# A decoder layer on one core: three turnings moved from TensorE to DMA, two bias rows moved from GpSimd to VectorE, and a new order inside the round

## The chip, the cores and the metric

The kernel runs on one core of one Trainium2 chip. The metric is the device time of the whole program in microseconds (us). The engines are named as the profile names them: PE is TensorE, DVE VectorE, ACT ScalarE, POOL GpSimd, and SP the engine that only issues DMAs. DMAs issued by SP travel in the queue called hardware_dynamic, those issued by POOL in software_dynamic; both are served by the same 16 DMA engines.

## The reference: what is computed

One post-norm decoder layer over x of 16 x 256 rows of 512 numbers: self-attention with 16 heads, cross-attention with one head of 64, then a mixture of 32 experts of which each token takes 8, with at most 512 tokens per expert.

```python
x = layernorm(x + attn(x))                    # softmax(q k^T / 8) v per head, then Wo, + bo
x = layernorm(x + xattn(ctx, ctx, x, mask))   # one head: out = softmax(q k^T / 8 - 1e9 mask) v; out @ Wo + bo
# experts
probs = softmax(x @ gate_weight.T); topw, topi = top_k(probs, 8); topw /= topw.sum(-1)
buf[e, pos] = x                               # up to 512 tokens for each expert
gate, up = split(buf @ gate_up_proj[e].T)     # 2 x 384
eo = (silu(gate) * up) @ down_proj[e].T
x = layernorm(x + sum over the 8 of topw * eo)
```

## The kernel before

Every matrix product is done in halves: a float32 number is written as a float16 high part plus a float16 low part (ACT makes the high part, DVE the low one, by `low` at L1107 to L1109, whose every use is profiled as L1109), and PE multiplies high with high, high with low and low with high, three products for one (`PARTS`, `split_mm` L508).

The program has two stages. The first is a software pipeline over the 16 batch elements, 19 rounds long (`rounds`, L330; rounds 4 to 14 are a loop on the engines, the others are written out). Round r works on four batch elements at once: b = r does q, k, v and the attention scores ("head"), t = r - 1 the rest of its heads, the projection and the first norm ("tail"), u = r - 2 the cross-attention and the second norm ("cross"), f = r - 3 the gate and the table of which token goes to which expert ("route"). So rounds 3 to 15 hold all four kinds of work, and rounds 16, 17 and 18 less and less. Each engine has its own `work` function with the whole round written out as eight steps of one head pair each; that order, by hand, is all the scheduling there is. An engine takes its instructions strictly in order, and a wait on a semaphore holds up all that stands behind it on that engine.

For a head pair j the chain is: `scores` (PE L550), `maxima` (DVE L1139), `exps` (ACT L863), `row_scales` (DVE L1145 and L1147), `probs_hi` (ACT L881), `probs_lo` (DVE, L1109 `stage<-arena_p`), `turn` (SP, two DMA transposes of 128 x 1024 float16, L402 and L404), `weigh` (PE L574), `heads_out` (ACT L853). The turning of the self-attention's probabilities and of x1 (`turn_x1`, L413 and L415) is done by DMA already. Three other turnings are done by PE against an identity matrix, out of float32: the cross-attention's probabilities (`cross_turn`, L623, 4 blocks of 128 x 128), x2 for the gate (`turn_x2`, L645, 8 blocks), and the gathered tokens of an expert (`turn_xg`, L775, 16 blocks). After each, ACT and DVE take the result out of PSUM as high and low half (`turned2_hi` L918 and `turned2_lo`; `x2_turned` L942 and `x2_lo`; `tokens_hi` L1057 and `tokens_lo`).

Two bias rows are added on POOL: `add_bias` (L1573, to xr, which holds the residual rows) and `add_bias2` (L1583, to x1). POOL's other work in a round is the low half of q and k (`qk_low`, L1564) and of the head outputs (`heads_lo`, L1568).

The second stage goes over the 32 experts. PE does `up_gate` (72 matmuls of 512 columns, L512), two blocks of `turn_xg` for the next expert, and `down` (36 matmuls, L786) with the two other blocks between its parts. POOL gathers the rows of expert e + 2 from x2_rows by indirect DMA (`gather`, L1654, 4 DMAs), and adds the 4 results of expert e into acc_rows by indirect DMA (`scatter`, L1660). SP loads the weights of expert e + 2 (`load_expert`, L418 and L420). The tokens of an expert stay in `xg` (two buffers, float32), their turned halves in `xgT` (one buffer, in `arena_v`). Before the first expert's matmuls PE does `turn_xg` four times with `keep_warm` matmuls (L678) between.

A third, short stage normalizes the 4096 rows.

## Time and profile before

| | us |
|---|---|
| median of 3 runs | 2085.09 (2084.96 to 2090.12) |
| the profiled execution | 2086.91 |
| its span in the profile | 2085.2 |
| PE, DVE, ACT, POOL busy in the span | 1879.4, 1421.7, 1258.3, 828.5 |
| mean granted clock of PE | 0.957 |

The span is the time from the first to the last instruction in the trace; about 1.7 us of the execution lie outside. Times inside the trace are us from the start of the span. The stage of rounds lasts until about 1214 us, the experts from about 1225 to 2037, and the last norm to the end. "Busy" is time with at least one instruction running; a busy engine can still be one that waits inside an instruction, for a port or an operand. The chain of work that ended last is 57% PE and 23% DVE, and PE is busy 90% of the span.

### The profile page before, as it was taken

What the parts mean: (1) busy time and instruction counts of PE and PEld (TensorE: products, weight loads), DVE (VectorE), ACT (ScalarE), POOL (GpSimd) and SP (SyncE); (2) the same over time, 40 slices, a digit from 0 to 9 for tenths busy, and PEclk for the clock granted to TensorE, in tenths of its full rate; (3) what the DMA queues carried; (4) which work ended last, traced back from release to release, by engine and by line L of the source; (5) the groups of instructions that cost most, each with busy time, mean ns of one, the idle gap of its engine ahead of it and who ended that gap; (6) DMA issues with size and microseconds to landing.
All of it is one profiled execution on the core that took longest, in us unless ns stands there. A gap on an engine that the chain in (4) does not pass through costs nothing.

```text
span 2085.2 us, 41762 instructions
## 1 busy us (share of the span) xinstructions
PE 1879.4 (90%) x14388; PEld 1113.9 (53%) x14388; DVE 1421.7 (68%) x2665; ACT 1258.3 (60%) x3119; POOL 828.5 (40%) x703
## 2 busy tenths in 40 slices
PE   6899999999999999999997559999999999999990
PEld 4556666566666665666564334444444444444440
DVE  5667898889888988898888655544555554555534
ACT  6877787778777877787776224444444444444434
POOL 1323332334233323332333135555555555555522
PEclk9999999999999999999998679999999999999995
DMA  7654554455445543554446157777777777777639
GB/s 214 127 99 104 109 128 111 90 112 125 106 91 112 122 111 81 122 122 109 86 111 143 51 176 220 178 178 178 178 176 175 180 180 189 189 189 179 130 46 336
DMA packets 418729, 295.26 MB, mean 142 GB/s; under 512 B 318704, under 2 KB 341232, under 8 KB 418672
## 3 DMA queue, kind: packets, MB, share of 16 engines
q1 hardware_dynamic: 389728, 224.26, 40.8%
q0 software_dynamic: 28944, 70.27, 18.2%
q8 instruction: 32, 0.52, 0.1%
q14 instruction: 25, 0.20, 0.0%
HBM read 158.67 MB, written 60.29 MB: 105 GB/s over the span
## 4 chain that ended last, share of the span: by engine, by line
PE 57%; DVE 23%; issue 10%; ACT 7%; DMA 1%; POOL 1%; DVEq 1%; ACTq 0%; SPq 0%; POOLq 0%
PE bank L512 39%; PE bank L786 12%; DVE stage L1109 7%; DVE s_neg L1139 5%; PE bank L775 3%; ACT arena_p L863 2%; PE bank L574 1%; DVE neg_l L1266 1%; PE bank L550 1%; ACT qk L843 1%; ACT arena_wo L1099 1%; DVE xt L1109 1%; DVE ct L1109 1%; DVE x1h L1109 1%; DVE stats L1175 1%
## 5 line engine op out<-in xcount | busy, mean ns | idle before, releaser
L512 PE MATMUL bank<-arena_v,arena_wo 128*128 128x512 f16 x2304 | 502.5, 379 | 0.6 <-PE bank L678 0.6
L512 PE MATMUL bank<-xt,arena_wo 128*128 128x256 f16 x3072 | 369.2, 278 | 18.8 <-DVE xt L1109 10.4
L512 PEld LDWEIGHTS bank<-arena_v,arena_wo 128*128 128x128 f16 x2304 | 225.3, 98 | 273.1 <-PE bank L678 1.5
L512 PEld LDWEIGHTS bank<-xt,arena_wo 128*128 128x128 f16 x3072 | 298.6, 100 | 84.5 <-issue 22.1
L1660 POOL DMA_INDIRECT acc_rows<-arena_wo,cur_to x128 | 202.4, 1581 | 308.3 <-ACT arena_wo L1079 276.9
L1109 DVE SCALAR_TENSOR_TENSOR arena_wo<-stage,arena_wo 128x3072 f16<-128x3072 f32 (+2 forms) x74 | 182.2, 2465 | 190.9 <-ACT arena_wo L936 174.9
L1564 POOL TENSOR_TENSOR qk<-qk 128x512 f16<-128x512 f32 x128 | 164.9, 1288 | 341.7 <-ACT qk L843 332.0
L863 ACT ACTIVATE arena_p<-bank,s_neg 128x256 f32<-128x256 f32 x512 | 236.2, 484 | 78.5 <-DVE s_neg L1139 78.5
L1109 DVE SCALAR_TENSOR_TENSOR stage<-arena_p,s_rden,stage 128x256 f16<-128x256 f32 x512 | 276.9, 600 | 5.7 <-ACT stage L881 5.7
L786 PE MATMUL bank<-arena_wo 128*128 128x512 f16 x1152 | 264.2, 379 | 0.7 <-DVE arena_wo L1511 0.7
L1568 POOL TENSOR_TENSOR arena_a<-o,arena_a 128x256 f16<-128x256 f32 x128 | 97.5, 762 | 384.9 <-ACT arena_a L853 383.9
L881 ACT ACTIVATE stage<-arena_p,s_rden 128x256 f16<-128x256 f32 x512 | 220.8, 527 | 36.8 <-DVE s_rden L1147 36.3
L1654 POOL DMA_INDIRECT arena_p<-x_rows,cur_from x128 | 214.9, 1679 | 56.2 <-issue 29.2
L843 ACT ACTIVATE qk<-bank,bqkv 128x256 f32<-128x256 f32 (+1 forms) x512 | 203.0, 502 | 44.6 <-PE bank L512 44.2
L1109 DVE SCALAR_TENSOR_TENSOR arena_v<-bank,arena_v 128x512 f16<-128x512 f32 x192 | 129.4, 687 | 105.2 <-ACT arena_v L1057 91.0
L1067 ACT ACTIVATE arena_a<-bank 128x512 f32<-128x512 f32 x96 | 57.0, 594 | 235.8 <-PE bank L512 235.8
L1079 ACT ACTIVATE arena_wo<-bank,cur_w 128x512 f32<-128x512 f32 x128 | 87.9, 687 | 162.2 <-PE bank L786 162.2
L512 PE MATMUL bank<-arena_wo,xt 128*128 128x512 f16 x768 | 178.0, 382 | 1.9 <-DVE arena_wo L1109 1.9
L1139 DVE TENSOR_REDUCE s_neg<-bank 128x2 f32<-128x512 f32 x256 | 163.7, 679 | 22.8 <-PE bank L550 22.8
L512 PE MATMUL bank<-arena_wo,arena_a 128*128 128x512 f16 x768 | 172.9, 382 | 2.2 <-POOL arena_a L1568 2.2
L786 PEld LDWEIGHTS bank<-arena_wo 128*128 128x128 f16 x1152 | 110.7, 98 | 117.9 <-DVE arena_wo L1511 10.4
L1504 DVE SCALAR_TENSOR_TENSOR arena_a<-bank,arena_a 128x512 f32<-128x512 f32 x96 | 65.9, 687 | 122.0 <-PE bank L512 121.7
(152 smaller groups left out, 2489.1 us busy)
## 6 DMA issues: line engine op xcount, KB each, us to landing
stage<-wguT SPq DMA_DIRECT2D x32, 1536.0 KB, 8.5
stage<-wdnT SPq DMA_DIRECT2D x32, 768.0 KB, 9.8
xt<-xT SPq DMA_DIRECT2D x16, 512.0 KB, 4.4
xr<-x_rows SPq DMA_DIRECT2D x16, 512.0 KB, 3.7
stage<-ctxT SPq DMA_DIRECT2D x16, 512.0 KB, 4.0
x_rows<-x SPq DMA_DIRECT2D x16, 512.0 KB, 2.9
acc_rows<-x SPq DMA_DIRECT2D x16, 512.0 KB, 3.7
arena_wo<-acc_rows SPq DMA_DIRECT2D x8, 1024.0 KB, 11.1
```

Source lines behind the costliest of these rows:

```text
L512: mm = pe.matmul(out_ap, lhs(a, i), rhs(c, i), start=(n == 0 and i == 0), stop=(n == 2 and i == chunks - 1))
L786: mm = pe.matmul(ps_y[c % 2][:, :], hT[:, a, f, c * P:(c + 1) * P], ew_dn[:, k, w, f, :], start=(f == 0 and n == 0), stop=(f == FC - 1 and ...
L843: ins = nc.scalar.activation(dst, ps_qk[:, at], ACT.Identity, bias=bqkv[:, w, j:j + 1], scale=scale / W_SCALE)
L863: ins = nc.scalar.activation(probs[:, j % 2, h, t, :], ps_s[h][:, t * S:(t + 1) * S], ACT.Exp, bias=s_neg[:, j % 2, n:n + 1], accum_out=s_ ...
L881: ins = nc.scalar.activation(p16[:, j % 2, 0, n * S:(n + 1) * S], probs[:, j % 2, n // TT, n % TT, :], ACT.Identity, scale=s_rden[:, j % 2 ...
L1079: nc.scalar.activation(y[:, k, c, :], ps_y[c % 2][:, :], ACT.Copy, scale=cur_w[:, k, c:c + 1]).then_inc(y_done, 1)
L1109: return vec.scalar_tensor_tensor(out=dst, in0=src, scalar=scale, in1=hi, op0=ALU.mult, op1=ALU.subtract)
L1139: vec.tensor_reduce(s_neg[:, j % 2, 2 * h:2 * h + 2], ps_s[h][:, :].rearrange("p (t k) -> p t k", t=TT), AX.X, ALU.max, negate=True).then_ ...
L1564: gp.tensor_tensor(qk[:, j % 2, 1, :], qk32[:, j % 2, :], qk[:, j % 2, 0, :], ALU.subtract).then_inc(qk_lo, 1)
L1568: gp.tensor_tensor(o[:, 1, j, :], o32[:, j % 2, :], o[:, 0, j, :], ALU.subtract).then_inc(o_lo, 1)
L1654: gp.indirect_dma_start(xg[:, k, c, :], None, x2_rows, bass.IndirectOffsetOnAxis(ap=cur_from[:, k, c:c + 1], axis=0)).then_inc(ld_xg[k], 16)
L1660: gp.indirect_dma_start(acc_rows, bass.IndirectOffsetOnAxis(ap=cur_to[:, k, c:c + 1], axis=0), y[:, k, c, :], None, compute_op=ALU.add).th ...
```

## The change

First, the three turnings on PE go. The data is split into halves before it is turned, lies as float16 in SBUF, and SP turns it with DMA transposes. For the cross-attention's probabilities ACT and DVE write `p2h` (128 x 512 each), SP turns it into `p2T` with 2 transposes of 4 blocks. For x2 they write `x2h`, and 2 transposes of 8 blocks make `x2T`. The rows of x2 are then stored to DRAM as halves (`x2_halves`), so that the gathered tokens are halves already, and 4 transposes of 8 blocks per expert turn them; ACT and DVE have nothing to split there. The turned tokens have two buffers (`xgT[k]`), and the results of `down` four PSUM banks where they had two. The `keep_warm` matmuls before the first expert go too. The division by the softmax sum of the cross-attention, a DVE pass over p2, is folded into the scale of the two splits.

```diff
-        xgT = arena_v[:, :].rearrange("p (s c n) -> p s c n", s=2, c=DC)
+        xg16 = arena_p[:, :].bitcast(F16).rearrange("p (b c n) -> p b c n", b=2, c=CC)
+        xgT = [arena[:, :].rearrange("p (c s d n) -> p c s d n", c=CC, s=2, d=DC) for arena in (arena_v, arena_q)]
...
-        ps_y = bank[6:8]
+        ps_y = bank[4:8]
...
+            def turn_halves(b, dst, src, done, free, free_at, landed):
...
+                sp.wait_ge(done[0], high)
+                past(sp, free, used)
+                sp.dma_start_transpose(dst[:, 0].rearrange("p t c n -> p (t c) n"), src[:, 0, :]).then_inc(landed, 16)
+                wait_apart(sp, done[1], count(b, 1, 1), ld_bias, 48)
+                sp.dma_start_transpose(dst[:, 1].rearrange("p t c n -> p (t c) n"), src[:, 1, :]).then_inc(landed, 16)
...
+            def turn_tokens(e, k, gathered):
+                landed, used = gathered, count(e - 1, FC)
...
+                sp.wait_ge(ld_xg[k], landed)
+                past(sp, u_mm, used)
+                for c in range(CC):
+                    sp.dma_start_transpose(xgT[k][:, c].rearrange("p s d n -> p (s d) n"), xg16[:, k, c, 0:2 * D])\
+                      .then_inc(ld_xgt[k], 16)
...
+            def tokens_then_weights(e, k, gathered):
+                turn_tokens(e, k, gathered)
+                next_but_one(e, 1 - k)
...
-            def expert(e, k, ahead, landed):
-                up_gate(e, k)
-                if ahead:
-                    pe.wait_ge(ld_xg[1 - k], landed)
-                    turn_xg(e + 1, 1 - k, 0)
-                    turn_xg(e + 1, 1 - k, 1)
-                down(e, k, ahead)
-
-            pe.wait_ge(ld_xg[0], 64)
-            for c in range(CC):
-                turn_xg(0, 0, c)
-                if c % 2:
-                    keep_warm(WARM[1])
+            def expert(e, k, landed):
+                up_gate(e, k, landed)
+                down(e, k)
...
+            def split_x2(b):
+                past(act, ld_x2t, count(b, 32))
+                past(act, st_x2, count(b, 48))
+                act.wait_ge(x2_done, count(b, TT, TT))
+                nc.scalar.activation(x2h[:, 0, :], x2[:, :, :].rearrange("p t n -> p (t n)"), ACT.Copy).then_inc(x2_hi, 1)
...
+            def split_p2(b):
+                dve.wait_ge(p2_hi, count(b, 1, 1))
                 for t in range(TT):
-                    ins = vec.tensor_scalar(p2[:, t, :], p2[:, t, :], rden2[:, t:t + 1], None, ALU.mult)
-                ins.then_inc(p2_done, 1)
+                    at = slice(t * S, (t + 1) * S)
+                    ins = low(p2h[:, 1, at], p2[:, t, :], p2h[:, 0, at], rden2[:, t:t + 1])
+                ins.then_inc(p2_lo, 1)
```

Second, the two bias rows. The same addition over 128 x 1024 float32 numbers is written for DVE in place of POOL.

```diff
+            def add_bias(b):
+                if isinstance(b, int) and b == 0:
+                    dve.wait_ge(ld_small, 32)
+                dve.wait_ge(ld_row, count(b, 16, 16))
+                vec.tensor_tensor(xr[:, :, :], xr[:, :, :], bo_row[:, :].unsqueeze(1).to_broadcast([P, TT, D]), ALU.add)\
+                   .then_inc(xb_done, 1)
+
+            def add_bias2(b):
+                past(dve, x1_lo, count(b, 1, 1))
+                vec.tensor_tensor(x1[:, :, :], x1[:, :, :], xbo_row[:, :].unsqueeze(1).to_broadcast([P, TT, D]), ALU.add)\
+                   .then_inc(x1b_done, 1)
```

Third, the order of the round on all engines, with the PSUM banks that go with it. On PE in the loop (the middle of a round, before): the turning of p stands behind the values' matmuls, and the pieces of the cross-attention lie between the two halves of the projection, `bank<-arena_wo,arena_a`.

```order
182 L512 MATMUL bank<-arena_wo,xt 128x512 x12
183 L620 REGISTER_ALU
184 L623 MATMUL bank<-ident,p 128x128 x4
185 L550 MATMUL bank<-qk 128x256 x12
186 L574 MATMUL bank<-arena_p,arena_v 64x256 x12
187 L52 REGISTER_ALU
188 L512 MATMUL bank<-xt,arena_wo 128x256 x24
189 L522 MATMUL bank<-p2T,v 64x256 x6
190 L588 REGISTER_ALU
191 L512 MATMUL bank<-arena_wo,arena_a 128x512 x24
192 L550 MATMUL bank<-qk 128x256 x12
193 L512 MATMUL bank<-wxo,o 128x512 x3
```

The same place after, where `arena_q` is the arena that now holds q and k:

```order
178 L586 MATMUL bank<-arena_q 128x256 x12
179 L610 MATMUL bank<-arena_p,arena_v 64x256 x12
180 L52 REGISTER_ALU
181 L548 MATMUL bank<-xt,arena_wo 128x256 x24
182 L548 MATMUL bank<-arena_wo,arena_a 128x512 x24
183 L586 MATMUL bank<-arena_q 128x256 x12
184 L548 MATMUL bank<-arena_wo,arena_a 128x512 x24
185 L604 REGISTER_ALU
186 L605 REGISTER_ALU
187 L610 MATMUL bank<-arena_p,arena_v 64x256 x12
188 L659 REGISTER_ALU
189 L558 MATMUL bank<-p2T,v 64x256 x6
```

There is no turning, and the product with p2T has moved behind the whole projection.

On ACT at the start of a round in the loop, before (`stage<-arena_p` are the high halves of the probabilities, `o<-bank` a head's output, `x1h` the high half of x1, `qk<-bank` what takes q and k out of PSUM):

```order
201 L826 ACTIVATE xt<-xt 128x1024
202 L878 ISA
203 L879 ISA
204 L881 ACTIVATE stage<-arena_p,s_rden 128x256 x4
205 L52 ISA
206 L851 REGISTER_ALU
207 L853 ACTIVATE o<-bank,bqkv 128x256
208 L853 ACTIVATE arena_a<-bank,bqkv 128x256
...
211 L889 ACTIVATE x1h<-x 128x1024
...
214 L863 ACTIVATE arena_p,s_den<-bank,s_neg 128x256 x4
...
217 L843 ACTIVATE qk<-bank,bqkv 128x256 x4
```

And after:

```order
200 L828 ACTIVATE xt<-xt 128x1024
...
203 L883 ACTIVATE stage<-arena_p,s_rden 128x256 x4
...
206 L865 ACTIVATE arena_p,s_den<-bank,s_neg 128x256 x4
...
209 L855 ACTIVATE o<-bank,bqkv 128x256
210 L855 ACTIVATE arena_a<-bank,bqkv 128x256
...
214 L947 ACTIVATE stage<-x 128x1024
...
217 L845 ACTIVATE arena_q<-bank,bqkv 128x256 x4
...
220 L891 ACTIVATE x1h<-x 128x1024
```

The exponentials come before the head's output, the split of x2 (`stage<-x`) is new and stands before what frees the PSUM bank of q and k, and the split of x1 has moved behind it.

On SP at the start of a round, after: the transposes of x2 stand between those of a head pair and those of x1.

```order
108 L404 DMA_TRANSPOSE arena_p<-stage 128x8x128
109 L406 DMA_TRANSPOSE arena_p<-stage 128x8x128
110 L412 ISA
111 L416 DMA_TRANSPOSE stage<-stage 128x8x128
112 L418 DMA_TRANSPOSE stage<-stage 128x8x128
113 L412 ISA
114 L416 DMA_TRANSPOSE x1T<-x1h 128x8x128
115 L418 DMA_TRANSPOSE x1T<-x1h 128x8x128
```

Before, the second pair of rows is not there.

## Rows read from the trace of the kernel before

**Rows 1.** Stretches: all experts but the edges, ten rounds; busy of each engine, clock, DMA

```profile
1231.00:2010.00 779.00, 779.00 (x3855) 382.02 (x3856) 401.64 (x465) 323.75 (x403) 425.86 (x334) 1.00 0.71 174
...
343.20:1043.50 700.30, 654.58 (x6510) 443.25 (x6507) 602.03 (x1291) 547.83 (x1662) 233.96 (x200) 0.99 0.49 109
```

**Rows 2.** Timeline of PE and SP's issues, two experts: start, us, what

```profile
1522.11 1.04 PE L775 MATMUL bank<-ident,arena_p 128*128 128x128 f32 x8
1522.98 2.11 PE L786 MATMUL bank<-arena_wo 128*128 128x512 f16 x9
...
1517.35 0.37 SPq L418 DMA_DIRECT2D stage<-wguT  x1
...
1542.42 0.37 SPq L418 DMA_DIRECT2D stage<-wguT  x1
```

**Rows 3.** DMA queues over one expert, 1506.57 to 1531.64: packets, MB, share of 16 engines

```profile
q0 software_dynamic: 896, 2.16, 47.8%
q1 hardware_dynamic: 928, 2.36, 26.6%
```

**Rows 4.** DMA queue from 613.5 to 616.5, one transpose alone

```profile
q1 hardware_dynamic: 1056, 0.26, 45.7%
```

**Rows 5.** DMA queues: 1507 to 1510 (scatter alone), then 1261 to 1264 (with loads)

```profile
q0 software_dynamic: 196, 0.37, 94.5%
...
q0 software_dynamic: 133, 0.25, 49.1%
```

**Rows 6.** Who PE waited for in ten rounds: us in total, times, longest

```profile
PE bank L623 <- DVE p L1224: 17.7, 10, 1.9
```

**Rows 7.** Timeline of PE, turnings in a round, and the clock from 656 to 660

```profile
621.44 1.04 PE L645 MATMUL bank<-ident,x 128*128 128x128 f32 x8
622.41 1.76 PE L671 MATMUL bank<-stage 128*32 128x16 f16 x64
...
655.64 0.66 PE L623 MATMUL bank<-ident,p 128*128 128x128 f32 x4 [1.94 <-DVE p L1224]
656.23 0.96 PE L550 MATMUL bank<-qk 64*128 64x256 f16 x12
...
656.00:660.00 4.00, 4.00 (x34) 2.52 (x33) 4.00 (x5) 4.00 (x10) 2.31 (x1) 0.60 0.84 197
```

**Rows 8.** Groups of DVE in ten rounds: busy, mean ns, idle before

```profile
L1109 DVE SCALAR_TENSOR_TENSOR x1h<-x,x1h 128x1024 f16<-128x1024 f32 x10 | 12.1, 1211 | 0.0
L1109 DVE SCALAR_TENSOR_TENSOR p2T<-bank,p2T 128x512 f16<-128x512 f32 x10 | 6.8, 680 | 0.0
L1224 DVE TENSOR_SCALAR p<-p,rden 128x256 f32<-128x256 f32 x20 | 6.2, 350 | 0.4
```

**Rows 9.** Timeline of DVE and POOL: where a POOL addition and DVE overlap

```profile
628.50 1.79 DVE L1109 SCALAR_TENSOR_TENSOR stage<-arena_p,s_rden,stage 128x256 f16<-128x256 f32 x4
...
631.67 2.21 DVE L1266 TENSOR_SCALAR neg_l<-top_l 128x2 f32<-128x2 f32 x1
...
644.41 4.18 DVE L1109 SCALAR_TENSOR_TENSOR stage<-arena_p,s_rden,stage 128x256 f16<-128x256 f32 x4
...
645.77 2.54 POOL L1573 TENSOR_TENSOR xr<-xr,bo_row 128x1024 f32<-128x1024 f32 x1
```

**Rows 10.** Issue to landing of a transpose; timeline of x1's two and their user

```profile
arena_p<-stage SPq DMA_TRANSPOSE x256, 3.1
...
631.88 1.24 SPq L413 DMA_TRANSPOSE x1T<-x1h  x1
633.28 1.24 SPq L415 DMA_TRANSPOSE x1T<-x1h  x1
...
639.10 0.85 PE L522 MATMUL bank<-x1T,wx 128*64 128x256 f16 x12
```

**Rows 11.** Start of the experts: timeline of PE, and its clock from 1225 to 1231

```profile
1224.96 1.97 PE L775 MATMUL bank<-ident,arena_p 128*128 128x128 f32 x8 [11.39 <-DMA arena_p<-x_rows,cur_from]
...
1225.00:1231.00 6.00, 5.39 (x21) 3.68 (x22) 2.92 (x5) 3.25 (x5) 2.83 (x7) 0.56 0.89 300
```

More of the change, by code:

```diff
@@ L637, in cross_project, with gate @@
                     .then_inc(out2_mm, 1)
-            def turn_x2(b, t, tail):
-                pe.wait_ge(x2_done, count(b, TT, t + 1))
-                if t and tail:
+            def gate(b, tail):
+                pe.wait_ge(ld_x2t, count(b, 32, 32))
+                if tail:
                     pe.wait_ge(ln1, count(b + 1, 7, 1))
-                for c in range(DC):
-                    mm = pe.transpose(ps_x2[t][:, c * P:(c + 1) * P], x2[:, t, c * P:(c + 1) * P], ident[:, :])
-                mm.then_inc(x2t_mm, 1)
@@ L704, in work @@
                     qk_pair(b, 2)
-                if route:
-                    positions(f)
+                    values(b, 1)
                 if cross:
```

432 lines of the change are left out of this document (194 added, 238 removed).

## The prediction

> **What bounds the kernel now.** I read the stretches first. In the 779 us of the experts PE is busy for 779 of 779 us at full clock, with DVE, ACT and POOL at about half and the DMA engines at 0.71 [rows 1]. So what PE is given there is the time, and nothing else is. In ten rounds (700.3 us, 70.03 each) PE is busy 654.6, DVE 602.0, ACT 547.8, POOL 234.0 [rows 1]: PE leads, with 4.57 us idle per round, and DVE is close behind at 60.2 per round. Then the waits of PE: 1.77 us per round for the scaled p that it turns [rows 6]. That hole costs more than itself: in the 4 us behind it the granted clock has a mean of 0.60, part of it at the lower of the two levels, 1.2 in place of 2.4 GHz [rows 7], and 4 x 0.40 = 1.6 us of work is lost. Then the timeline of DVE beside that of POOL: the same four probability splits take 1.79 us alone and 4.18 us when POOL's addition to xr (2.54 us) runs beside them, and a neg_l of 128 x 2 numbers takes 2.21 us where POOL adds the other bias row [rows 9]. The 4.18 stand ahead of the masking, and so of the hole. Last the DMA queues, since that is where the work goes.
>
> **The experts.** Eight turnings start at 1522.11 and the next product at 1522.98: 0.87 us [rows 2]. 16 per expert make 1.74 us. The period is 1542.42 - 1517.35 = 25.07 us [rows 2]; without the turnings 23.33. There are 31 such sets between the experts (the first expert's is in the start, below): 31 x 1.74 = -53.9 us. ACT and DVE lose four passes each; they had half their time free, so that is worth nothing.
>
> Does something else become late? Each expert gets 4 transposes of 256 KB. One alone takes 0.457 x 3 x 16 = 21.9 engine-us, four 87.7 [rows 4]. Today one expert takes (0.478 + 0.266) x 25.07 x 16 = 298 [rows 3]. The sum, 386, over 16 engines is 24.1 us, and this is above 23.33. But POOL's packets are long because they wait alone: 0.945 x 48 us / 196 = 231 ns for one of the scatter with the queue to itself, and 0.491 x 48 / 133 = 177 ns where weight loads run beside it [rows 5]. If the 192 engine-us of that queue shrink in that proportion to 147, the sum is 342 or 21.3 us, under 23.33. So bounds 23.33 and 24.1; I take 23.33, since the engines, once short of time, are in the mixed state. Late arrivals are forgiven: the gather of expert e + 2 is issued early in expert e, its transposes may start when e's 72 matmuls are done, and they are needed one expert later, with two buffers. SP issues them at 1.40 us spacing [rows 10], 5.6 us of 23.3, and its load of the next weights, which it issues once per expert, comes between them without waiting for more than today. For POOL's gather the wait on a landed turning is for one issued an expert before.
>
> The Trainium skill (Advanced Engine Details and Errata, X-Bar Transpose (TRN2)) says that transposing DMAs are as fast as regular ones. Rows 3 and 4 do not agree: 2.36 MB of weights take 107 engine-us, 45 per MB, a transpose 84 per MB. By the rule the four would cost about 47 and the experts' sum without any shrinking would be 345, 21.6 us; by the rows the case is close.
>
> **The rounds.** PE loses 4 turnings of p (656.23 - 655.64 = 0.59 us) and 8 of x2 (0.97) [rows 7]: 1.56. With the hole's clock loss of 1.6 gone, PE's work is 65.46 - 1.56 - 1.6 = 62.3 us: the floor. Idle today is 4.57, of which 1.77 is the wait for the turned p. In the new order the product with p2T stands behind the whole projection and one head pair; from the end of the splits two transposes need 1.40 + 3.1 = 4.5 us [rows 10], and the projection's second half and a pair's work lie over them, so I count no wait. The other 2.8 us stay. I add 1.0 for ACT: its new split of x2 (the size of DVE's 1.21 [rows 8]) stands ahead of what empties the only bank of q and k, and PE's values no longer stand behind the first q and k, so the second must wait for the bank. 62.3 + 2.8 + 1.0 = 66.1 us against 70.03: -3.9. Bounds: 62.3, and 68.5 if all the idle time and the clock loss come back elsewhere (62.3 + 4.57 + 1.6).
>
> DVE decides whether that holds. It loses 0.68 for p2T, two of that size for x2, and 0.62 for the scaling [rows 8]: 2.7. It gains a split of x2 (1.21), two of the four splits of 1.79 us for p (0.9), a scaling of two numbers (under 0.35) and two additions of 128 x 1024. No row has these on DVE: the nearest from below is the split of the same size, 1.21, from above POOL's 2.54; I take 1.2 each, the row of the same engine. Sum +4.7. And the stalls beside POOL's additions go: 4.18 - 1.79 = 2.4, and 2.21 against at most the 0.35 of the much larger scaling [rows 8], 1.9: -4.3, down to 0 if POOL's remaining work hits DVE instead. The edits come to +2.0, so DVE ends at 60.2 + 2.0 - 4.3 = 57.9, at the worst (2.54 each, no stall back) at 64.9. At 57.9 it covers; at 64.9 the round is some 68. On SP each round gets 4 transposes more, 5.6 us; x1's two now come behind x2's two, 2.8 us later. They landed by 633.28 + 3.1 = 636.4 and were needed at 639.10 [rows 10]: 2.7 of slack, and the gate and a block of values now stand ahead of that product.
>
> Rounds 2 to 15 have this work in full or nearly: 14 x -3.9 = -55 us. POOL's queue gets shorter; that hides nothing.
>
> **Start and tail.** The first gather lands at 1224.96, and PE's own turning and warm-up lasted until about 1231, at a mean granted clock of 0.56 [rows 11]. After: four issues and a landing, 3 x 1.40 + 3.1 = 7.3, so matmuls from 1232.3, +1.3; and they begin after 19 us without work, so at the lower level, as the turnings did. The half speed then falls on matmuls, for about the 6 us of that row: 6 x 0.44 = +2.6. Together +4. In rounds 16 to 18 nothing covers the transposes: for p about 4.5 us of DMA replace PE, ACT and DVE passes (0.59, and two of the size of 0.68, with gaps), roughly +2 twice, for x2 +1.5 twice, less 1.2 twice for the addition that DVE does faster than POOL: +4.
>
> **Sum.** Against the profiled execution, 2086.9 (span 2085.2 and 1.7 around it): 2086.9 - 53.9 - 55 + 4 + 4 = 1986. The median shown is 1.8 lower: **1984 us**, 4.8% less.
>
> **Rivals.**
> A, the rounds keep their time. DVE is at its worst, or ACT's new order makes PE wait for the bank or for the exponentials what it saves. For it: DVE is 86% busy, and each engine now has its pieces in an order in which one late piece holds up the next head pair. Against: the stalls it loses are in the rows. 1984 + 55 = 2039 us.
> B, the DMA engines set the experts' pace without shrinking: 24.1 us and some gaps, up to 24.8. 31 x 0.8 to 1.5 = +25 to +46, so about 2020.
> C, x1T is late: its transposes behind x2's, and both splits later in ACT and DVE than I laid them. 2.8 us per round, 14 x 2.8 = +39: 2023.
> D, slower than before: transposes of 256-byte packets get slower beside scatter and gather rather than these shorter. The experts lose once the four cost more than 25.07 x 16 - 298 = 103 engine-us, 26 each against 21.9 alone; only 19% more. At half as much again (33 each) the engines need 430, 26.9 us: +1.8 x 31 = +56 where I have -54, so 1984 + 110 = 2094; to be over 2085 they must reach 32. For it: so many packets; against: the mixed rows.
> E, the floor is reached in the rounds (62.3 to 64): 1984 - 14 x 3 = 1942.
>
> The Trainium skill (VectorE: DVE Perf Modes, The three transpose paths and its rules for kernel authors) gives 390 ns for a 128 x 128 block on TensorE and 1309 ns by DMA, and advises TensorE where the result may be in PSUM. It speaks against the change. The trace shows the same sign for latency (3.1 us for a transposing DMA, 0.11 of PE per block), but where PE is full its 0.11 is what counts; taken as it stands, the rule would have the change at best in case A or C.
>
> **How the numbers follow.** Forecast 0.52 (1965 to 2005), A 0.12, B 0.11, C 0.08, D 0.09, E 0.08. The range 1945 to 2050 leaves out most of D and part of E, with the worse part of A and B: 0.2. About 0.3% is what a measurement can tell from no change: faster 0.88, same 0.03, slower 0.09, D with a small part of A and B together as "same".
>
> **What would show it.** Right: in the experts PE busy all the time at full clock and the weight loads 23.3 us apart; DMA share near 0.9 to 0.95; rounds of 65 to 67 us; neg_l back under 0.35 us and no split of 4 us; PE's wait for turned p gone, at most small ones before the second q and k and the exponentials. Wrong: PE waiting for `xgT` (B, D); a POOL packet that has not become shorter; PE waiting for x1T (C), or DVE over 64 us busy in a round (A).

## The result and the profile after

The changed kernel takes 2040.9 us (2036.19 to 2044.33, four runs) where the kernel before takes 2085.95 in the same comparison: a ratio of 0.9774, interval 0.9763 to 0.9786. Faster, as forecast, but by 45 us and not by 101; 2040.9 lies in the range. It is near the time of rival A by chance: A has the rounds keep their time, but half of what is missing was lost in the experts. The profiled execution took 2036.19 with a span of 2034.1 us.

| part | before | forecast | after |
|---|---|---|---|
| one expert, load to load | 25.07 | 23.33 | 24.16 |
| one round (issue of xr to issue of xr) | 69.90 | 66.1 | 67.93 |
| PE busy in a round | 65.5 | 62.3 | 63.6 |
| end of the last slots matmul to first expert matmul | 17.4 | 18.7 | 23.8 |

The stretches of the changed kernel, ten rounds and then 600 us of experts, answer to [rows 1]; the columns are the same (busy time and instructions of PE, PE's weight loads, DVE, ACT, POOL, then the clock, the DMA share and GB/s):

```profile
286.80:966.10 679.30, 635.91 (x6378) 432.33 (x6377) 564.19 (x1299) 546.75 (x1657) 177.57 (x179) 0.99 0.57 124
1300.00:1900.00 600.00, 583.69 (x2687) 260.72 (x2685) 257.42 (x272) 210.68 (x224) 377.97 (x275) 1.00 0.97 230
```

DVE is at 56.4 us per round, under the 57.9 of the forecast. PE, busy without a gap among the experts before, now idles 16.3 us in 600. The waits of PE tell what for. First the experts (1200 to 1990; us in total, times, longest), and then the ten rounds:

```profile
PE bank L548 <- DMA arena_v<-arena_p: 23.8, 1, 23.8
PE bank L802 <- DVE arena_wo L1509: 21.7, 32, 0.7
```

```profile
PE bank L586 <- ACT arena_p L865: 24.9, 20, 2.1
PE bank L548 <- ACT arena_q L845: 13.4, 10, 1.3
PE bank L548 <- DVE xt L1098: 2.8, 10, 0.3
```

The one wait for turned rows is the start, 23.8 us. The other is new: 0.68 us in each of 32 experts, in front of `down`'s products with the last third of h (the 384 rows of an expert's hidden values h are handled as three blocks, f = 0, 1, 2). The timeline of PE and of SP's issues over one expert shows its place, and the period (24.15 us here, 24.16 in the mean):

```profile
1465.17 1.46 PE L802 MATMUL bank<-arena_wo 128*128 128x512 f16 x6
1467.30 6.65 PE L802 MATMUL bank<-arena_wo 128*128 128x512 f16 x30 [0.68 <-DVE arena_wo L1509]
...
1460.42 0.38 SPq L441 DMA_DIRECT2D stage<-wguT  x1
1469.51 7.46 SPq L437 DMA_TRANSPOSE arena_v<-arena_p  x4
...
1484.57 0.38 SPq L441 DMA_DIRECT2D stage<-wguT  x1
```

`down` needs h of the last f, and its low half is ready some 2 us after the last up matmul. Before, eight turnings lay between them [rows 2]. The trace of before had this hole in PE's work too, in its last expert, which has no next one to turn:

```profile
2025.38 6.65 PE L786 MATMUL bank<-arena_wo 128*128 128x512 f16 x30 [0.68 <-DVE arena_wo L1511]
```

The DMA queues of the changed kernel over one expert, 1460.42 to 1484.57, against [rows 3]:

```profile
q1 hardware_dynamic: 5152, 3.41, 61.3%
q0 software_dynamic: 903, 2.19, 40.0%
```

POOL's packets take 0.400 x 24.15 x 16 us / 903 = 171 ns, where before they took 0.478 x 25.07 x 16 / 896 = 214. They shrank, as the forecast had it. The other queue has 237 engine-us; less the 107 of the weights [rows 3], that leaves 32 per transpose, against 21.9 alone [rows 4], if the weights cost what they did. Both queues overlap to a share of about 1, yet no expert but the first waits for a transpose.

In the rounds the two long stalls on DVE are gone and the additions cost what I took. These are DVE's neg_l, a set of its four splits of p and its two additions, against 2.21 and 4.18 us in [rows 9]:

```profile
553.10 0.17 DVE L1267 TENSOR_SCALAR neg_l<-top_l 128x2 f32<-128x2 f32 x1
...
564.21 1.68 DVE L1098 SCALAR_TENSOR_TENSOR stage<-arena_p,s_rden,stage 128x256 f16<-128x256 f32 x4
...
566.09 1.22 DVE L1162 TENSOR_TENSOR x<-x,xbo_row 128x1024 f32<-128x1024 f32 x1
...
578.64 1.22 DVE L1157 TENSOR_TENSOR xr<-xr,bo_row 128x1024 f32<-128x1024 f32 x1
```

PE still waits 4.1 us in a round (4.3 with the smallest gaps), with other waits than in [rows 6]. The largest is ahead of scores(2), the scores of head pair 2. Its chain, read from PE back to ACT and to DVE's routing choice (whose last instruction is w), with what POOL does beside w:

```profile
565.54 0.83 PE L586 MATMUL bank<-arena_q 64*128 64x256 f16 x12 [1.97 <-ACT arena_p L865]
...
561.24 1.71 ACT L883 ACTIVATE stage<-arena_p,s_rden 128x256 f16<-128x256 f32 x4 [1.21 <-DVE s_rden L1136]
...
559.78 1.07 DVE L1292 SCALAR_TENSOR_TENSOR w<-pr,w_rsum 128x64 f32<-128x64 f32 x1
560.78 0.17 DVE L1134 RECIPROCAL s_rden<-s_den 128x4 f32<-128x4 f32 x1
```

```profile
559.62 1.16 POOL L1556 TENSOR_TENSOR arena_q<-arena_q 128x512 f16<-128x512 f32 x1 [2.61 <-ACT arena_q L845]
```

So one stretched DVE instruction is left in this chain. w takes 1.07 us in all ten rounds, and 0.23 in the last round, where POOL has nothing beside it; here it ends where POOL's low half of q and k ends. The kernel before had the same (w 1.04 us). No run parted the two.

The clock did not come back whole either. Ten us around the wait before scores(2), in two rounds that follow each other (the clock is the third figure from the end):

```profile
495.00:505.00 10.00, 8.29 (x60) 5.29 (x61) 7.94 (x23) 9.64 (x34) 2.55 (x3) 0.83 0.45 85
...
565.00:575.00 10.00, 9.46 (x74) 5.72 (x75) 8.37 (x23) 10.00 (x34) 2.57 (x3) 1.00 0.52 98
```

The first round has a dip to the lower level behind that wait, the second has none. Five of the ten rounds have one, and they take 68.6 to 69.0 us; those without take 67.2 to 67.5, the first of the ten 65.9.

### The profile page after: what moved, and what is told of

The parts are those of the page before. It is cut to its first block, busy times and chain, and to the rows that moved or that the text cites. A ratio compares the mean times of both kernels' runs of the same rounds, so it can differ in the third digit from the quotient of the medians.

```text
span 2034.1 us, 40256 instructions
## 1 busy us (share of the span) xinstructions
PE 1793.0 (88%) x13680; PEld 1034.9 (51%) x13680; DVE 1283.1 (63%) x2553; ACT 1192.3 (59%) x2991; POOL 766.5 (38%) x669
## 4 chain that ended last, share of the span: by engine, by line
PE 54%; DVE 17%; ACT 15%; issue 9%; DMA 2%; SPq 1%; POOL 1%; DVEq 1%; ACTq 0%; POOLq 0%
PE bank L548 40%; PE bank L802 10%; ACT arena_p L865 4%; DVE stage L1098 3%; ACT stage L883 3%; ACT arena_q L845 3%; DVE s_neg L1128 2%; PE bank L586 2%; PE bank L610 1%; ACT arena_wo L1088 1%; DVE arena_wo L1509 1%; DVE arena_a L1502 1%; ACT arena_a L855 1%; DVE ct L1098 1%; DVE xt L1098 1%
## 5 line engine op out<-in xcount | busy, mean ns | idle before, releaser
L1556 POOL TENSOR_TENSOR arena_q<-arena_q 128x512 f16<-128x512 f32 x128 | 168.6, 1317 | 370.9 <-ACT arena_q L845 354.5
L802 PE MATMUL bank<-arena_wo 128*128 128x512 f16 x1152 | 259.4, 379 | 21.7 <-DVE arena_wo L1509 21.7
L548 PE MATMUL bank<-arena_v,arena_wo 128*128 128x512 f16 x1152 | 253.5, 381 | 23.8 <-DMA arena_v<-arena_p 23.8
L1560 POOL TENSOR_TENSOR arena_a<-o,arena_a 128x256 f16<-128x256 f32 x128 | 91.2, 712 | 455.8 <-ACT arena_a L855 455.8
L1098 DVE SCALAR_TENSOR_TENSOR stage<-arena_p,s_rden,stage 128x256 f16<-128x256 f32 x512 | 230.8, 510 | 39.8 <-ACT stage L883 39.8
L548 PE MATMUL bank<-arena_q,arena_wo 128*128 128x512 f16 x1152 | 251.3, 379 | 0.0
L845 ACT ACTIVATE arena_q<-bank,bqkv 128x256 f32<-128x256 f32 (+1 forms) x512 | 203.9, 507 | 55.4 <-PE bank L548 55.4
L883 ACT ACTIVATE stage<-arena_p,s_rden 128x256 f16<-128x256 f32 x512 | 221.0, 532 | 16.3 <-DVE s_rden L1136 16.3
L548 PEld LDWEIGHTS bank<-arena_v,arena_wo 128*128 128x128 f16 x1152 | 113.2, 98 | 161.3 <-DMA arena_v<-arena_p 23.9
L1632 POOL DMA_INDIRECT arena_p<-x_rows,cur_from x128 | 164.6, 1286 | 56.4 <-issue 29.0
L548 PEld LDWEIGHTS bank<-arena_q,arena_wo 128*128 128x128 f16 x1152 | 112.7, 98 | 135.9
```

Of the source, the lines that this page charges most:

```text
L548: mm = pe.matmul(out_ap, lhs(a, i), rhs(c, i), start=(n == 0 and i == 0), stop=(n == 2 and i == chunks - 1))
L802: mm = pe.matmul(ps_y[c][:, :], hT[:, a, f, c * P:(c + 1) * P], ew_dn[:, k, w, f, :], start=(f == 0 and n == 0), stop=(f == FC - 1 and n = ...
L845: ins = nc.scalar.activation(dst, ps_qk[:, at], ACT.Identity, bias=bqkv[:, w, j:j + 1], scale=scale / W_SCALE)
L883: ins = nc.scalar.activation(p16[:, j % 2, 0, n * S:(n + 1) * S], probs[:, j % 2, n // TT, n % TT, :], ACT.Identity, scale=s_rden[:, j % 2 ...
L1098: return vec.scalar_tensor_tensor(out=dst, in0=src, scalar=scale, in1=hi, op0=ALU.mult, op1=ALU.subtract)
L1556: gp.tensor_tensor(qk[:, j % 2, 1, :], qk32[:, j % 2, :], qk[:, j % 2, 0, :], ALU.subtract).then_inc(qk_lo, 1)
```

## The experiments

Each was timed beside the kernel before, whose median was 2085.5 us beside e1 to e4, 2088.1 beside e5 to e8, 2087.83 beside e9 to e11 and 2087.06 beside e12 to e15. Periods come from the profiled runs: of a round from ten rounds between SP's issues of xr, of an expert from its weight loads or from PE's first matmul.

| run | us | ratio (interval) | round | expert |
|---|---|---|---|---|
| changed kernel | 2040.9 | 0.9774 (0.9763-0.9786) | 67.93 | 24.16 |
| e1 down's order | 2011.23 | 0.9668 (0.9625-0.9711) | 67.87 | 23.31 |
| e2 quarter turned | 2065.33 | 0.9903 (0.9887-0.992) | | 24.38 |
| e3 scales first | 2041.73 | 0.978 (0.9763-0.9797) | 67.85 | |
| e4 x2 after qk | 2042.03 | 0.9788 (0.9772-0.9804) | 68.16 | |
| e5 ring first | 2014.13 | 0.9648 (0.9632-0.9664) | 67.47 | |
| e6 half the turning | 2011.33 | 0.9634 (0.9618-0.965) | 67.94 | 23.31 |
| e7 biases on POOL | 2080.9 | 0.9969 (0.9959-0.9979) | 71.39 | |
| e8 biases alone | 2027.18 | 0.9708 (0.9692-0.9724) | 65.69 | |
| e9 ring then qk | 2024.31 | 0.9701 (0.9685-0.9717) | 68.55 | |
| e10 norm later | 2007.11 | 0.9619 (0.9603-0.9635) | 67.09 | |
| e11 start too | 2003.24 | 0.9599 (0.958-0.9618) | 67.13 | |
| e12 values back | 2011.45 | 0.9643 (0.9627-0.9659) | 67.44 | |
| e13 and norm later | 1995.73 | 0.9588 (0.9552-0.9624) | 65.94 | |
| e14 and x2 early | 1986.44 | 0.9532 (0.951-0.9554) | 65.70 | |
| e15 with start | 1987.64 | 0.9552 (0.9503-0.9601) | 65.75 | |

**e1, down's order.** The changed kernel, with `down` beginning on the two thirds of h that are ready, for two of its four blocks of rows c:

```diff
-for c in range(CC):
-    for f in range(FC):
+order = [(0,0), (1,0), (0,1), (1,1), (0,2), (1,2)] + [(c,f) for c in (2,3) for f in range(FC)]
+for c, f in order:
```

> The changed kernel with one edit: in down, PE does the first and second third (f = 0, 1) of both c = 0 and c = 1 before the last third of either, so 12 matmuls (2.6 us) stand between up_gate and the first use of h's last third, where the changed kernel has 6 (1.3 us). Theory H: the turnings on PE had covered the way from the last up_gate matmul over ACT's silu and DVE's three passes to h's last low half, and their removal uncovers a hole of 0.68 us per expert; it goes: experts 23.48 us apart, 32 x 0.68 = 22 us less than the changed kernel, about 2019 us, ratio to before 0.968. Rival D: the DMA engines, 0.97 busy in the experts, are what sets 24.16 us; then the period stays near 24.1, a wait for the turned tokens takes the hole's place, and the ratio stays 0.977.

The hole is gone. Experts of e1, 600 us of them, and PE over one expert:

```profile
1300.00:1900.00 600.00, 600.00 (x2781) 272.02 (x2780) 268.23 (x284) 215.00 (x232) 359.08 (x286) 1.00 1.02 239
```

```profile
1526.42 7.93 PE L803 MATMUL bank<-arena_wo 128*128 128x512 f16 x36
1534.19 15.70 PE L548 MATMUL bank<-arena_v,arena_wo 128*128 128x512 f16 x72
```

The period is 23.31, the forecast's 23.33, with PE full and the DMA engines at 1.02. So the lost 0.85 us per expert was this hole: 0.68 shown as idle and 0.17 of the pipeline that empties ahead of it (7.93 us for the 36 matmuls against 1.46 + 0.68 + 6.65 with their overlap at the ends). 31 x 0.85 = 26 us, which is the difference of the two spans (2034.1 and 2008.0).

**e2, a quarter of the turnings.** The kernel before, with one block of four turned for every group of rows (three quarters of the rows' columns are left out of the computation):

```diff
-for d in range(DC):
+for d in range(1):   # all but the first expert
```

> The kernel before with one edit: of the 16 blocks that PE turns per expert (from the second expert on) it turns only 4, one per group of rows; the other three quarters of the tokens are left out of the turning. No DMA is added. By the sum of the prediction this is worth 12 x 0.109 = 1.3 us per expert, 31 times, 40 us, ratio 0.981. Theory H says that 0.65 us of it fall on the 2 blocks-groups between up_gate and down, which cover the last low half of h: 6 matmuls and 2 blocks give 1.5 us where about 2.0 to 2.15 are needed, so a hole of 0.5 to 0.65 us per expert opens, and only about 0.7 to 0.8 us per expert remain: 23 us, ratio 0.989, experts 24.3 us apart with full DMA slack.

```profile
1465.99 0.82 PE L786 MATMUL bank<-arena_wo 128*128 128x512 f16 x3 [0.46 <-DVE arena_wo L1511]
```

Twelve of the sixteen blocks are worth 12 x 0.109 = 1.31 us of PE, but the period falls only by 0.69, to 24.38: the hole opens in the kernel before as soon as the turnings shrink. The row shows 0.46 us of it; with the same 0.17 for the emptying pipeline as in e1 it is 0.63, and e1's 23.31 with that and four turnings (0.44) makes 24.38, as measured.

**e3 and e4, single moves in the changed kernel.** e3 put the scaling of pair 0 ahead of the routing's choice on DVE, e4 ACT's and DVE's split of x2 behind the copy of the first q and k:

```diff
e3 (DVE)                          e4 (ACT; DVE alike)
-if route: choose(f)              -if route: split_x2(f)
 pair(row_scales, 0)               if head: qk_out(b, 0)
+if route: choose(f)              +if route: split_x2(f)
```

> The changed kernel with one edit: on DVE the row scales of pair 0 stand ahead of the choice of the experts (choose, 11 small operations, some 3.2 us), which in the changed kernel stands ahead of them. Theory O: ACT's high halves of pair 0 wait 1.2 us for those scales, behind them stand the exponentials of pair 1, and PE waits 1.97 us for them at the scores of pair 2. The wait goes nearly whole: rounds of 66.0 to 66.5 us in place of 67.93, 14 x 1.6 = 22 us, about 2019 us, ratio 0.968. Rival: the hole is DVE's total load, not its order; then the scores' wait moves to another place and the rounds stay within 0.4 us of 67.93.

> The changed kernel with one edit: ACT's split of x2 stands behind the taking out of the first q and k instead of before it, and DVE's split of x2 behind the row scales. Theory O: PE's wait of 1.34 us per round for the bank of q and k is that split's 1.08 us; it falls to about 0.3: rounds of 66.9, 14 x 1.0 = 14 us, about 2027 us, ratio 0.971. Rival C: x2T and x1T, turned later by the same amount, are late for the gate and the cross-attention's q, the wait moves there and nothing is won (ratio 0.977).

Neither changed the time: both rivals held. In e3 ACT started the high probabilities 1.2 us earlier, but then waited 1.17 us for the maxima, which still stood behind the choice. In e4 the waits for ACT fell, and PE waited for transposes instead (ten rounds of e4, their stretch first):

```profile
289.60:971.20 681.60, 645.06 (x6375) 433.94 (x6373) 566.23 (x1298) 552.38 (x1658) 179.86 (x180) 0.97 0.57 124
```

```profile
PE bank L558 <- DMA x1T<-x1h: 17.6, 10, 1.8
PE bank L548 <- DMA stage<-stage: 5.8, 10, 0.7
PE bank L586 <- ACT arena_p L865: 4.9, 10, 0.5
PE bank L548 <- ACT arena_q L845: 3.9, 10, 0.4
```

So case C of the prediction lies just behind the order as it is: with the splits 1.6 us later on ACT, x1T is late. But PE idles only 3.7 us in a round of e4, against 4.3 in the changed kernel. What took the gain back is the clock: every round now has a dip, behind the wait for x1T, and PE is busy for 64.5 us in place of 63.6 with the same work.

**e5, the ring first.** The ring is scores, maxima (DVE), exps (ACT), and the next scores into the bank that the exps empty. On the kernel of e1:

```diff
DVE: row_scales(0), maxima(1)                       ACT:  +exps(1)
     ahead of values_lo(1) and choose                      heads_out(-2)
                                                           probs_hi(0)
                                                          -exps(1)
```

> The kernel with down's order from e1, and in the step of the second scores the ring scores, maxima, exps goes ahead: on VectorE the maxima(1) stand before the low half of the values and the routing's choice, on ScalarE the exps(1) stand before the heads of pair -2 and the high probabilities of pair 0. Theory R: the hole of 2.0 us that TensorE has in every full round before scores(2) is made by 3.4 us of choice and 0.7 us of low half that stand ahead of the maxima, and by 2.6 us of ScalarE's work ahead of the exps; e3 moved only a scaling of 0.4 us and left the choice ahead of the maxima, so it gained nothing. Then the hole goes, a round takes 66.0 to 66.5 instead of 67.9 us, and the time is 1985 to 1992. Rival S: ScalarE and VectorE are so full that the wait comes back at the next scores or at the turned probabilities: a round stays over 67.3, 2003 to 2015.

The wait before scores(2) went, and one of nearly that size came at the next product, which needs q and k's bank:

```profile
574.94 2.79 PE L548 MATMUL bank<-xt,arena_wo 128*128 128x256 f16 x24 [1.59 <-ACT arena_q L847]
```

Rival S holds, with 67.47 a round. PE's waits are no shorter than in e1 (4.1 us in a round in both); the 0.4 us are the clock's, since no round of e5 has a dip. The first rounds lost 8 us besides, so that the profiled execution is 4 us longer than e1's (2014.23 and 2010.1).

**e6, half the turning.** e1 with only the high halves turned; the matmuls take the high half in the place of the low one.

> The kernel of e1 with only the high halves of the gathered rows turned, and the high half taken in the place of the low one in the matmuls (a part of the computation left out): half of the transposed bytes in every expert, the same matmuls. Theory: in e1 TensorE is busy in 600 of 600 us of experts, so the DMA engines at a share of 1.02 do not set the pace and a period stays 23.3; what shrinks is the start, where the turning stands between the gathers and the first matmul with 10.6 us to land: to 6 or 7 us, 2005 to 2008 against e1's 2011. Rival B (DMA engines at their limit cost time somewhere in the experts' loop): a period under 23.2, over 5 us below the start's gain, under 2000.

No change: the experts stay 23.31 us apart with PE busy in 600 of 600 us, though the DMA share fell to 0.89. None at the start either. The first four transposes with half the bytes took 1196.33 to 1205.6, against 1195.28 to 1205.1: it is not their size that they wait for. Rival B is out; my 3 to 6 us for the start were wrong as well.

**e7 and e8, the two halves of the change apart.** e7 is the changed kernel with the two additions back on POOL, e8 the kernel before with only the two additions on DVE, in the same steps of the round as in the changed kernel.

> The changed kernel with the two bias rows added by GpSimd again, at their places of the kernel before; everything else as changed. By the sum of the prediction the DVE instructions that stood beside GpSimd's additions were stretched by 2.2 and 4.2 us in a round and TensorE waited for them: if that was worth time, a round is 1 to 2.5 us longer, 2055 to 2075. Rival W: TensorE's wait of 4.3 us in a round is set by the ring of scores, maxima and exps with the choice in it, which no bias touches: within 5 us of the changed kernel's 2041.

> The kernel before with only the biases moved to VectorE, as the changed kernel has them; TensorE still turns. VectorE gains two additions of 1.2 us in a round and loses the stretching beside GpSimd. By the sum: a round shorter by what it made TensorE wait, up to 2 us, 2060 to 2080. Rival W: no more than 3 us either way, 2083 to 2089. Rival D: the additions on VectorE stand ahead of maxima, a round longer by 0.5 to 1, 2092 to 2100.

e8 beats the whole change: 61 us under before against 45, and e7, all the rest, has 7. Both effects are over what I expected (28 us at most for e8, 34 for e7 over the changed kernel). Ten rounds of e8 and e7, then the two large PE waits of before in its ten rounds, then those of e8 and of e7:

```profile
286.60:943.60 657.00, 643.33 (x6502) 439.26 (x6500) 564.27 (x1310) 547.26 (x1660) 186.53 (x180) 1.00 0.52 116
```

```profile
288.20:1002.10 713.90, 646.54 (x6378) 437.30 (x6377) 581.90 (x1278) 547.03 (x1658) 228.69 (x200) 0.96 0.54 118
```

```profile
PE bank L550 <- ACT arena_p L863: 18.2, 10, 1.8
PE bank L623 <- DVE p L1224: 17.7, 10, 1.9
```

```profile
PE bank L512 <- DVE slots L1345: 4.9, 10, 0.5
PE bank L512 <- DVE xt L1109: 3.7, 10, 0.4
PE bank L512 <- POOL arena_a L1582: 2.1, 10, 0.2
PE bank L550 <- ACT arena_p L863: 1.7, 10, 0.2
```

```profile
PE bank L586 <- ACT arena_p L865: 48.8, 20, 4.9
PE bank L548 <- ACT arena_q L845: 13.4, 10, 1.3
```

| a round, us (PE busy + idle) | biases on POOL | on DVE |
|---|---|---|
| old order, PE turns | 69.90 (65.5 + 4.4) | 65.69 (64.3 + 1.4) |
| new order, DMA turns | 71.39 (64.7 + 6.7) | 67.93 (63.6 + 4.3) |

The additions' move is worth 3.5 to 4.2 us in a round in either order: 2.4 to 3.0 of waits, and 1.1 to 1.2 of PE's busy time, though PE's work is the same; that part is the clock (0.96 and 0.99 in the new order, 0.99 [rows 1] and 1.00 in the old). The rest of the change costs 1.5 to 2.2. It does take about 1.5 us of work off PE: e14 below, like e8 at a clock of 1.00, is busy for 62.9 us in a round, where e8 has 64.3. But in the changed kernel 0.7 of that goes to its dips in the clock, and 3.0 us of idle time come on top. In e8 no wait of PE is over 0.5 us: the two large ones of before (1.8 before a scores, 1.9 before the turned p) went with the additions, as the DVE instructions of [rows 9] that had been stretched beside them did, and the clock rose to 1.00. In e7 the stretched one stands inside the choice, here POOL's addition and DVE's w (1.95 us at the median of ten rounds, for the 0.23 without POOL beside it), and PE's wait behind it:

```profile
576.06 2.35 POOL L1551 TENSOR_TENSOR xr<-xr,bo_row 128x1024 f32<-128x1024 f32 x1 [2.28 <-DMA xr<-x_rows]
```

```profile
576.54 1.94 DVE L1281 SCALAR_TENSOR_TENSOR w<-pr,w_rsum 128x64 f32<-128x64 f32 x1
```

```profile
583.94 0.83 PE L586 MATMUL bank<-arena_q 64*128 64x256 f16 x12 [4.50 <-ACT arena_p L865]
```

The Trainium skill (SBUF — State Buffer, Who interferes with whom) says that DVE's second pair of ports is GpSimd's too, and that a use of it locks the other engine out. The trace agrees as far as the times go: 1.94 us for one of 0.23, and w ends 0.07 us behind the addition beside it.

**e9 to e11, on the ring again.** e9 moves qk_out(3) ahead of the high probabilities in e5; e10 puts DVE's norm1 of a block behind the next round's first maxima, where the kernel before and the changed one have it at the end of a round; e11 adds the start: the second gather behind the first turning, and 14 idle matmuls on PE.

```diff
e10 (DVE)                         e11 (POOL; on PE keep_warm(14) before expert 0)
-if tail: norm1(t)    # round's end       -gather(1, 1)
 ...                                       column_out(0, 0)
 pair(maxima, -2); pair(probs_lo, -3)     +pool.wait_ge(ld_xgt[0], 64)
+if cross: norm1(u)   # next round        +gather(1, 1)
```

> As e5, but on ScalarE the copy of the next queries and keys, qk_out(3), stands between the heads of pair -2 and the high probabilities of pair 0 (the first round keeps its old order, since e5 lost 8 us there). e8 showed a round of 65.7 with the biases on VectorE and TensorE still turning, 2.2 less than the changed kernel's 67.9, though TensorE works 0.7 more in it: theory O says that those 2.2 and more are made by the new order of the rounds, not by turning by DMA. e5 took the wait of 2.0 us before scores(2) away and got 1.6 us back at qk_pair(4), behind 1.7 us of high probabilities. By theory O that wait goes too: a round takes 65.8 to 66.3, 1982 to 1990. Rival S: ScalarE is late again one step on, a round stays over 67.2, 2000 to 2012.

> As e9, and VectorE's normalization of the first residual (two instructions, 1.0 to 1.9 us) moved from the end of a round to the start of the next, behind the maxima of pair -2. By theory O the 0.5 and 1.3 us that TensorE waits at a round's border come from exps that wait 2.55 us for these maxima: a round of 64.2 to 64.8, 1958 to 1970, TensorE's waits under 1.2 us in a round. Rival: the low half of x1, and with it cross_q, comes late instead: no change against e9 or up to 1 us a round worse.

> As e10, and between the rounds and the experts: the gather of the second expert is issued only when the turning of the first has landed, and TensorE does 14 idle matmuls while the first is turned (the kernel before had such matmuls there). e6 halved the bytes turned and the four transposes still took 9.3 us from first issue to landing, against 9.8, so bytes are not what they wait for. If it is the second expert's gather and the weights on the same engines, the start shortens by 3 to 5 us, and the first 72 matmuls take 15.7 in place of 17.2 to 18.6: 4 to 7 us under e10. Rival: the transposes cost 2 us each to issue whatever runs beside them: 1 to 2 us from the clock alone.

e9 missed: 68.55 a round, worse than e1, and rival S holds. The wait moved on once more, to the low half of a head on POOL and to o, the output of the cross-attention:

```profile
647.45 5.35 PE L548 MATMUL bank<-arena_wo,arena_a 128*128 128x512 f16 x24 [1.24 <-POOL arena_a L1567]
664.18 1.47 PE L548 MATMUL bank<-wxo,o 128*128 128x512 f16 x6 [1.34 <-DVE o L1103]
```

e10 took 1.46 off, as forecast, though from e9's higher level, so its 67.09 misses the 64.2 to 64.8. e11 took 3.9 us off e10 (2003.24 and 2007.11), just under the 4 to 7 expected: the first expert started 3.8 us earlier, with all 72 matmuls at full clock,

```profile
1199.07 15.70 PE L548 MATMUL bank<-arena_v,arena_wo 128*128 128x512 f16 x72 [2.60 <-issue]
```

and 2.4 came back at the fifth expert, whose turning was late.

**e12 to e15, the filler put back.** On e1, the second quarter of the values (12 matmuls, 2.75 us) goes behind qk_pair(3), with its copies, where the kernel before has it (e12); norm1 as in e10 (e13); ACT's high half of x2 at the end of the round (e14); the start of e11 (e15):

```diff
e12 (PE; ACT and DVE alike)       e14 (ACT)
 qk_pair(b, 2)                    -if route: split_x2(f)    # before qk_out(0)
-values(b, 1)                      ...
 ...                               qk_out(b, 7)
 qk_pair(b, 3)                    +if cross: split_x2(u)    # end of the round
+values(b, 1)
```

> The kernel of e1 with the second quarter of the values, 2.75 us of TensorE, and its two copies put back one step later, where the kernel before and e8 have them (behind qk_pair(3)). Theory V: in the changed order TensorE has 8.0 us of work in one step and 4.5 in the next, while ScalarE has 6 to 7 in each and is busy without a gap from 545 to 560 us of the trace; so the wait of 2.0 us before scores(2) is the lack of this filler, and e5 and e9, which only reordered ScalarE and VectorE, pushed it on to the next step. Then the 2.0 go; up to 1.5 come back before scores(1), since ScalarE is late there already: a round of 66.4 to 67.4 (67.9 in e1), 1991 to 2004. Rival: it is the count of instructions on ScalarE: 67.8 or more, 2010.

> As e12, with VectorE's normalization of the first residual behind the next round's first maxima, as in e10, where it took 1.5 us off a round (67.1 after 68.6). By theory V the exps start 1.9 us earlier and ScalarE with its whole queue: 1.3 to 2.0 us off e12's round, 65.0 to 65.9, 1972 to 1984. If the gain of e10 belonged to its order alone: as e12.

> As e13, with ScalarE's copy of x2 to its high half, 1.1 us, at the end of a round, where ScalarE was idle for 2.5 us, in place of the next round's start, where it stands ahead of qk_out(0) and TensorE waits 1.3 us for that. By theory V another 0.7 to 1.1 us off a round, 64.1 to 65.0, 1960 to 1972. Rival: x2 is not normalized by then, ScalarE waits for it at the end of the round and carries the wait on: 0 to 1 us a round worse than e13.

> As e14, with the start of e11 (the second gather behind the first turning, 14 idle matmuls). e11 took 3.9 us off e10: 3 to 5 us under e14. No part is left out, so that this is the fastest complete version if theory V holds.

e12's round of 67.44 is just over the forecast's 67.4, and its time is the rival's: no time gained over e1. The 2.0 us before scores(2) are gone, and 1.54 stand before scores(1), where ACT was late already. PE's waits in a round are as long as in e1; the 0.4 us less are again the clock's, 1.00 in e12. With that, norm1's move took 1.5 off (65.94, and a median of 1995.73 that misses the forecast's 1984), as in e10; 1.3 of it are waits in both. e14 took a further 0.24 only, below its forecast, and its profiled execution (1986.78) is no shorter than e13's (1986.64); the copy ahead of q and k went, and x1T and the exps kept part of it. PE's waits in ten rounds of e14:

```profile
PE bank L586 <- ACT arena_p L867: 15.9, 28, 1.2
PE bank L558 <- DMA x1T<-x1h: 5.4, 10, 0.7
PE bank L548 <- ACT arena_q L847: 3.9, 10, 0.4
```

e14 has 62.87 us of PE busy in a round (628.7 in ten), near the 62.3 that the forecast called the floor, and is 100.6 us under before in its comparison. That is the gain forecast for the change, but by moves that the change does not have. e15, forecast 3 to 5 us under e14, cannot be told from it (1982.52 to 2005.17).

## Why the prediction was off

**Experts, -53.9 forecast, -28 measured** (31 x 0.91). The first step that failed is "31 x 1.74 = -53.9 us", from a period of 25.07 now and "without the turnings 23.33". The 1.74 us of work were right, and e1 reaches 23.31. But the first eight turnings covered PE's wait for the last low half of h, of which the sum knew nothing: "busy for 779 of 779 us" says that nothing waits while the turnings are there. With them gone 0.68 + 0.17 us per expert were late next. It was to be read in one row of before, the last expert's. e1 and e2 show it from both sides. The sign "PE busy all the time at full clock" was wrong for the same reason.

**DMA engines** (rivals B and D). The step held: packets of POOL's queue shrank from 214 to 171 ns, PE never waited for a turned expert in the middle, and e6 shows that half the turned bytes change nothing. The share was 0.97 where I put 0.9 to 0.95. The transposes themselves got slower, to about 32 engine-us by the difference, past the 26 at which rival D starts to lose; D fell only since its price held the packets beside them at their old size.

**Rounds, -3.9 forecast, -2.0 measured**, 14 x 1.9 = 27 us lost. The forecast's 66.1 is 62.3 of work and 3.8 of waits; measured are 63.6 and 4.3. The second step that failed is thus above all "With the hole's clock loss of 1.6 gone", a loss taken from a single dip. In that trace the dip comes only in every second round, as the same 4 us show one round ahead and one behind those of [rows 7]:

```profile
586.00:590.00 4.00, 3.59 (x42) 2.83 (x43) 3.97 (x8) 4.00 (x12) 2.31 (x1) 1.00 0.69 161
...
726.00:730.00 4.00, 3.56 (x41) 2.79 (x42) 3.97 (x7) 4.00 (x12) 2.31 (x1) 1.00 0.70 152
```

The other seven rounds of these ten keep to that turn, and the rounds take 69.2 and 70.8 us by turns. So there were 0.8 us per round to win by these rows, or 1.2 by e8, which has PE's same work at a clock of 1.00. And the changed kernel has dips of its own in five of ten rounds, 0.7 per round against e14. Of the waits ("The other 2.8 us stay. I add 1.0 for ACT") the sum was nearly right and the reasons were not. e7 and e8 part them: with the additions moved only 1.4 us of the old idle time were left (e8); the new order brings 3.0 of its own. So the forecast gave the turnings in the rounds the credit of the additions, and charged the reordering nothing but 1.0. Rival A, "ACT's new order makes PE wait for the bank or for the exponentials what it saves", is the mechanism of the waits, at half its price. Rival C did not come, but e4 shows it 1.6 us away.

What in the new order does it is open in part. PE's values(1), the second quarter of the values, had been the work of the step in which PE now waits; ACT has 6 to 7 us in each step there, with x2's split, the gate's exps and the masked exps besides; and DVE's norm1, splits and slots stand ahead of the first maxima. Four orders that touch this (e3, e5, e9, e12) left PE's waits as long or made them longer, and e4 exchanged them for a slower clock. Only norm1's move shortened them, by 1.3 us in a round on e9 and on e12 alike. But norm1 stands at the end of a round in the kernel before and in e8 too, so its move is a gain beyond the old order and does not say what the new one costs. It was tried neither on e1 nor on e8 alone. PE in e13 still waits 1.5 for ACT before scores(1), at which e8 has 0.2, and what of that is x2's split and what p2's is open.

**Start and tail, +4 and +4 forecast.** The start cost +6.5 to the first matmul, where the forecast had +1.3, and 2.3 for 72 matmuls at part of the clock (17.96 us against 15.70), where it had 2.6: +8.7 in all. Failed: "four issues and a landing, 3 x 1.40 + 3.1 = 7.3". It took 10.6, from SP's timeline and PE's:

```profile
1195.11 8.52 SPq L437 DMA_TRANSPOSE arena_v<-arena_p  x4
...
1205.73 17.96 PE L548 MATMUL bank<-arena_v,arena_wo 128*128 128x512 f16 x72 [23.84 <-DMA arena_v<-arena_p]
```

Another 1.8 us lie ahead of it: the first turning began 13.2 us behind the last slots matmul, where PE's began 11.4 behind it in the kernel before; why is not shown. The 7.3 hold when the second gather is not on the DMA engines: e6 rules out the bytes turned, and in e11, where that gather comes later, it is 7.3 us from the first issue (1191.75) to the first matmul. e11's 72 matmuls take 15.70 us again behind its idle matmuls, where e10's take 17.83. The tail, from the last issue of xr to the last slots matmul, gave -1.4 where +4 was forecast; no run says why.

**Right**: the sign, DVE's 56.4 in a round, the price of 1.2 for the additions, the stalls that went, no wait for turned p, and nearly the load on the DMA engines.

## What to carry to other kernels

Work taken off a full engine is worth its time less what waited behind it: look for the place where the trace already lacks that work (a last or first iteration), since the next wait stands there in plain figures. Before a change of two parts is credited to one, do each alone: here a move of two additions, 2.4 us of DVE in a round, was worth more than all the rest with it. Where an order is rewritten, read the idle time and the busy time of PE apart: e5 and e12 shifted a wait without shortening it, and what they won was the clock, while e4 shortened PE's waits and lost it to the clock. And a loss of clock seen once is to be looked up in the rounds beside it before it is put into a sum.

## What the runs showed of the hardware

- A DMA engine share of 1.02 to 1.04, as the profile counts it over 600 us, went with no waiting of PE at all (e1, e5).
- Issuing four transposes on SP took 5.4 us for the first expert of e11, with the second gather held back, mostly 7.4 to 10.3 among the experts of the changed kernel, and 18 to 20 for its second and third, where gathers, scatters and two weight loads meet; what is behind them on SP is held up as long.
- A 128 x 1024 addition of two f32 tiles took 1.22 us on DVE and 2.35 to 2.54 on POOL, and while POOL had it, a DVE instruction of 0.2 us took up to 2.2 (neg_l before, w in e7: up to 2.35). Beside POOL's low half of q and k (1.16 us) w took 1.04 to 1.07.
- A wait of PE of 1.9 to 2.1 us was followed by a dip of the granted clock in five of ten rounds (before, changed kernel), by none in the others. In e4 the dip came in every round, behind a wait of 1.8.
